# Who issues the stores of new v into the ring: SyncE or ScalarE

## The chip, the cores and the metric

The kernel runs on one core of a Trainium2 chip. Its engines are TensorE (PE, with its weight loads PEld), VectorE (DVE), ScalarE (ACT), GpSimd (POOL) and SyncE (SP, which computes nothing and issues DMAs). Each engine takes its own instructions in order; between engines a semaphore is incremented by one instruction and waited for by another. The metric is the device time of one execution in microseconds.

## The reference, cut to what matters

Four layers run one after the other on 16 sequences of 256 tokens and 128 channels: a gated recurrence, a mixture of experts, a linear attention, and a six-layer local attention transformer. The last one is the part that the change touches and nearly all of the time. Each of its six layers does this:

```
def attn_layer(x, Wqkv, qs, ksc, Wo):
    q, k, v = jnp.split(x @ Wqkv, 3, -1)            # 16 heads of 64
    q, k = l2norm(q) * qs, l2norm(k) * ksc          # then both are rotated
    ...
    out = local_attention(q, k, v)                  # window of 32, and the window before
    return out @ Wo

def local_attention(q, k, v):
    bk2, bv2 = look(bk), look(bv)                   # this window's keys and values, and the last one's
    sim = jnp.einsum('bhwie,bhwje->bhwij', bq, bk2) * QK_SCALE
    attn = jax.nn.softmax(jnp.where(mask, -big, sim), -1)
    return jnp.einsum('bhwij,bhwje->bhwie', attn, bv2)
```

A feed-forward layer with a GELU gate follows each attention layer.

## The kernel before

The tokens are cut into 8 windows of 32. A unit u is one window of one layer (48 units), a group n is one unit's share of four sequences, 128 rows (192 groups). One loop over groups, written once per engine, is a software pipeline: in round n the engines project q, k and v of group n (`proj`, six matmul groups into PSUM banks), score group n-2 (`sim`), take exponents of n-3 (`exps`), turn probabilities and multiply by values of n-4 (`probs`, `values`), and project the output of n-5 (`out_proj`). The feed-forward work of an earlier unit is spread over the four rounds of a unit; q4 = n % 4 says which pieces stand in a round. The order on each engine is written out by hand; nothing is reordered by a scheduler.

The keys and values of the current and the previous window lie in a ring. The ring of v is `V2` in `big1`: the rows of one window lie at partitions 64*par + 32*(c % 2), where par is the parity of the head and c the window. The projection of v gives 128 rows in which the four sequences lie below one another, so v has to move across partitions. ACT copies each half of it from PSUM into the staging tile `vst` (`v_out(n, par)`, L1255), which increments the semaphore a_vst, and four DMAs of 32 partitions by 2 KB each (L340) carry it from `vst` into `V2`. They increment d_v of the group's place in the unit. `values` waits for these DMAs four rounds later, and the next group's first `v_out` waits for them before it overwrites `vst`.

On ACT the part of a round around it is: `v_out(n, 0)`, `square(n, 2)`, `turned_k(n - 2, 0)`, `square(n, 3)`, `turned_k(n - 2, 1)`, `out_turned(n - 4, 0)`, `v_out(n, 1)`, and at the start of the next round `out_turned(n - 4, 1)`, in one round of four a GELU, the two `turned_q(n, h)` (L1262), and then squares and `probs` copies in turn. PE's order in a round is: `turn_q` of the round before, `proj(n, 0)`, `probs(n - 4, 0)` (L592), `proj(n, 1)`, `probs(n - 4, 1)`, `out_proj`, feed-forward pieces, `values` (L608), `proj(n, 4)` (the first half of v), `proj(n, 2)`, `turn_k`, `proj(n, 3)`, `turn_k`, `mask`, `proj(n, 5)`, `sim` (L581), `turn_q(n, h)` (L546). Banks 2 and 3 are shared by v, the turned q and k and the probabilities, so each user waits until ACT has emptied the bank for the one before: `probs(n - 4, 0)` takes bank 3 after `turned_q(n - 1, 0)` has read it.

SP issues all other loads of this stage too: rotation tables once per unit (L323), and new weights once per layer into `stage` (L336, L343), which ACT and DVE split into a high and a low part (`weights`, L1240).

Of the kernel before, what the change touches and what calls it, by code (L numbers as in the profile page):

```python
# [16 lines left out]
NC, W = 8, 32  # L17
N = NB * W
DEPTH, HEADS, DH = 6, 16, 64
# [7 lines left out]
TURN = (0, 1, 4, 2, 3, 5)  # L27
# [124 lines left out]
def program(nc, x_d, kc_d, wa_d, wb_d, ba_d, tab_d, qs_d, wqkv_d, wo_d, w1_d, w2_d, vec_d, we_d, out_d, keep_d, xsort_d, ysort_d):  # L152
    with ExitStack() as ctx:
# [11 lines left out]
        stage = sb("stage", [P, 2, 512])  # L165
# [21 lines left out]
        vst = sb("vst", [P, 2, 512])  # L187
# [28 lines left out]
        s = sems  # L216
# [33 lines left out]
        V2 = big1[:, :].rearrange("p (b n) -> p b n", b=NB)  # L250
# [17 lines left out]
        def _(eng):  # L268
            q = Lane(eng, sems)
# [14 lines left out]
            for what, c, j in chunk_order("SP"):  # L284
# [14 lines left out]
                elif what == "wt" and j < 4:  # L299
                    q.wait_ge("v_w", j + 1)  # L300
                    m = TURN[j + 2]
# [8 lines left out]
            for n in range(NG + 32):  # L310
                u, i = n // 4, n % 4
                l, c = unit(u)
                if n < NG:
                    if n % 32 == 5 and n > 32:
                        q.wait_ge("p_wo", n - 5)
                        eng.dma_start(wo[:, :, :], wo_d[l]).then_inc(s["d_wo"], 16)
                    if i == 0 and u + 1 < NU:
                        if c == NC - 1:
                            q.wait_ge("g_tab", u - NC + 1)
                            eng.dma_start(qsb[:, (l + 1) % 2, :, :], qs_d[l + 1]).then_inc(s["d_qs"], 16)  # L320
                        q.wait_ge("v_k", 16 * u)
                        q.wait_ge("g_tab", u)
                        eng.dma_start(tab[:, (u + 1) % 2, :, :], tab_d[(u + 1) % NC]).then_inc(s[f"d_tab{(u + 1) % 2}"], 16)  # L323
                    if n % 32 == 8 and l + 1 < DEPTH:
                        q.wait_ge("v_w", 6 * (l + 1))
                        for j in range(2):
                            m = TURN[j]
                            eng.dma_start(stage[:, j, :], wqkv_d[l + 1, :, 512 * m:512 * m + 512]).then_inc(s[f"d_st{j}"], 16)
                    q.wait_ge("p_av", n - 3)
                    q.wait_ge("g_zero", 2)  # L330
                    for par in range(2):
                        if n % 32 == 31 and l + 1 < DEPTH:
                            for j in (0, 1) if par == 0 else (2,):
                                m = TURN[j + 2]
                                q.wait_ge("v_w", 6 * (l + 1) + j + 1)
                                eng.dma_start(stage[:, j % 2, :], wqkv_d[l + 1, :, 512 * m:512 * m + 512]).then_inc(s[f"d_st{j % 2}"], 16)  # L336
                        q.wait_ge("a_vst", 2 * n + par + 1)
                        rows = 64 * par + 32 * (c % 2)
                        for b in range(4):
                            eng.dma_start(V2[rows:rows + 32, 4 * i + b, :], vst[32 * b:32 * b + 32, par, :]).then_inc(s[f"d_v{i}"], 16)  # L340
                    if n % 32 == 31 and l + 1 < DEPTH:
                        q.wait_ge("v_w", 6 * (l + 1) + 4)
                        eng.dma_start(stage[:, 1, :], wqkv_d[l + 1, :, 512 * TURN[5]:512 * TURN[5] + 512]).then_inc(s["d_st1"], 16)  # L343
                if n % 32 == 24 and l + 1 < DEPTH:
                    q.wait_ge("v_w1", l + 1)
                    eng.dma_start(w1, w1_d[l + 1]).then_inc(s["d_ffn"], 16)
                if n % 32 == 16 and 32 < n < NG:
                    q.wait_ge("p_fw", 8 * l)
                    eng.dma_start(w2, w2_d[l]).then_inc(s["d_down"], 16)
                v = u - 3  # L350
                if i == 0 and NU - NC <= v < NU:
                    q.wait_ge("v_w", 6 * DEPTH)
                    q.wait_ge("v_back", v - (NU - NC) - 1)
                    q.wait_ge("d_keep", 16 * NC)
                    eng.dma_start(stage[:, v % 2, :], keep_d[:, v % NC, :]).then_inc(s[f"d_back{v % 2}"], 16)
                v = u - 7
                if i == 0 and NU - NC <= v < NU:
                    q.wait_ge("v_out", v - (NU - NC) + 1)
                    eng.dma_start(out_d[:, v % NC, :], Xr[:, v % NC, :]).then_inc(s["d_out"], 16)
# [769 lines left out]
        def _(eng):  # L1129
            ac = Lane(eng, sems)  # L1130
# [26 lines left out]
            for n in range(2):  # L1157
                rows = slice(W * n, W * n + W)
                eng.activation(idb[rows, :].rearrange("p (b t) -> p b t", b=4), kc[rows, rows].unsqueeze(1).to_broadcast([W, 4, W]), ACT.Copy,
                               scale=1.0, bias=0.0).then_inc(s["a_mb"], 1)  # L1160
            for what, c, j in chunk_order("ACT"):
# [30 lines left out]
                elif what == "tx":  # L1192
                    n = 4 * c + j
# [4 lines left out]
                elif what == "he":  # L1198
                    k, m = PR * c + j, 256 * min(2, TL - 2 * j)
# [28 lines left out]
                elif what == "wt":  # L1228
                    m = TURN[j]
# [19 lines left out]
            def v_out(g, par):  # L1249
                if not 0 <= g < NG:  # L1250
                    return
                ac.wait_ge("p_proj", 6 * g + TURN.index(4 + par) + 1)
                if g:
                    ac.wait_ge(f"d_v{(g - 1) % 4}", 128 * ((g - 1) // 4 + 1))
                eng.activation(vst[:, par, :], bank[RING["v"][par]][:, :], ACT.Copy, scale=1.0, bias=0.0).then_inc(s["a_vst"], 1)  # L1255

            def turned_q(g, h):
                if not 0 <= g < NG:
# [426 lines left out]
```

## Time and profile before

| | |
|---|---|
| median of 3 runs | 3699.72 us (3698.93 to 3707.35) |
| the profiled execution | 3692.47 us |
| its span, first to last instruction | 3690.6 us |
| around the span | 1.87 us |
| PE busy | 3457.5 us, 94% |
| POOL busy | 2814.9 us, 76% |
| DVE busy | 2807.4 us, 76% |
| ACT busy | 2365.4 us, 64% |
| mean granted TensorE clock | 0.972 |

The profiled execution is 7.3 us (0.2%) below the median of the runs. Busy time counts work on the engine; instructions that wait or issue DMAs are not counted as busy. The attention loop runs from about 590 us to the end of the span; the first of the 384 v copies starts at 589.5 us and the last one, the second of its round and some 3.5 us into it, at 3563.6 us. Between them lie 191 rounds, so a round takes (3563.6 - 3.5 - 589.5) / 191 = 15.55 us.

### The profile page before, as it was taken

What the parts mean: (1) busy time and instruction counts of PE and PEld (TensorE: products, weight loads), DVE (VectorE), ACT (ScalarE), POOL (GpSimd) and SP (SyncE); (2) the same over time, 40 slices, a digit from 0 to 9 for tenths busy, and PEclk for the clock granted to TensorE, in tenths of its full rate; (3) what the DMA queues carried; (4) which work ended last, traced back from release to release, by engine and by line L of the source; (5) the groups of instructions that cost most, each with busy time, mean ns of one, the idle gap of its engine ahead of it and who ended that gap; (6) DMA issues with size and microseconds to landing.
All of it is one profiled execution on the core that took longest, in us unless ns stands there. A gap on an engine that the chain in (4) does not pass through costs nothing.

```text
span 3690.6 us, 148973 instructions
## 1 busy us (share of the span) xinstructions
PE 3457.5 (94%) x64612; PEld 2724.5 (74%) x64612; DVE 2807.4 (76%) x4876; ACT 2365.4 (64%) x4307; POOL 2814.9 (76%) x3470
## 2 busy tenths in 40 slices
PE   4799986999999999999999999999999999999996
PEld 2566644888877888787888778887787877888774
DVE  3487666888887888878888878888788888788762
ACT  3333223677777777777777677777677777777662
POOL 1455547998878888888888788888888888888761
PEclk9799997999999999999999999999999999999998
DMA  3323302211112111111111211111111112111110
GB/s 106 99 89 95 91 24 58 50 40 38 46 49 50 39 42 42 49 42 45 41 40 45 50 50 38 43 42 49 43 46 40 44 40 57 38 43 47 36 37 24
DMA packets 126733, 183.48 MB, mean 50 GB/s; under 512 B 29824, under 2 KB 61440, under 8 KB 126080
## 3 DMA queue, kind: packets, MB, share of 16 engines
q1 hardware_dynamic: 119232, 146.15, 15.8%
q0 software_dynamic: 6848, 27.80, 2.5%
q8 instruction: 511, 8.37, 1.0%
q14 instruction: 142, 1.16, 0.1%
HBM read 59.01 MB, written 14.16 MB: 20 GB/s over the span
## 4 chain that ended last, share of the span: by engine, by line
PE 84%; POOL 5%; DVE 3%; issue 3%; ACT 2%; DMA 1%; SPq 0%; ACTq 0%; POOLq 0%; DVEq 0%
PE bank L536 22%; PE bank L608 10%; PE bank L619 9%; PE bank L581 7%; PE bank L546 5%; PE bank L556 4%; PE bank L592 4%; PE bank L682 3%; PE bank L660 3%; PE bank L671 3%; PE bank L568 2%; PE bank L451 1%; PE bank L511 1%; PE bank L628 1%; PE bank L490 1%
## 5 line engine op out<-in xcount | busy, mean ns | idle before, releaser
L536 PE MATMUL bank<-wqkv,xs 128*128 128x512 f32 x3456 | 1060.9, 422 | 17.2 <-DVE m L957 12.9
L1540 POOL TENSOR_TENSOR m<-m 128x512 f32<-128x512 f32 x576 | 728.7, 1285 | 42.0 <-DVE m L957 39.2
L536 PEld LDWEIGHTS bank<-wqkv,xs 128*128 128x128 f32 x3456 | 582.7, 191 | 146.4 <-issue 57.2
L957 DVE TENSOR_TENSOR m<-bank,tab 128x512 f32<-128x512 f32 x768 | 522.4, 680 | 0.7 <-POOL m L1540 0.3
L1247 ACT ACTIVATE sq<-bank 128x512 f32<-128x512 f32 x768 | 458.5, 597 | 96.9 <-PE bank L536 53.3
L1548 POOL TENSOR_TENSOR S<-S,nw 128x1024 f32<-128x1024 f32 x192 | 383.3, 1996 | 166.0 <-DVE S L988 166.0
L968 DVE TENSOR_REDUCE ss<-sq 128x8 f32<-128x512 f32 x768 | 505.7, 675 | 0.0
L1556 POOL TENSOR_TENSOR S<-S,rs 128x512 f32<-128x512 f32 x384 | 411.0, 1091 | 63.8 <-DVE rs L1002 62.2
L608 PEld LDWEIGHTS bank<-P,big 64*64 64x64 f32 x24576 | 379.3, 135 | 82.0 <-issue 74.6
L955 DVE TENSOR_TENSOR m<-bank,tab 128x512 f32<-128x512 f32 x576 | 392.6, 682 | 56.3 <-ACT sq L1247 41.1
L619 PE MATMUL bank<-OT,wo 128*128 128x128 f32 x3072 | 389.1, 282 | 39.3 <-ACT P L1286 25.9
L608 PE MATMUL bank<-P,big 64*64 64x32 f32 x24576 | 402.1, 220 | 5.0 <-issue 3.8
L1255 ACT ACTIVATE vst<-bank 128x512 f32<-128x512 f32 x384 | 229.6, 598 | 273.2 <-PE bank L536 258.8
L619 PEld LDWEIGHTS bank<-OT,wo 128*128 128x128 f32 x3072 | 370.6, 197 | 43.1 <-issue 42.8
L1262 ACT ACTIVATE qT<-bank 128x512 f32<-128x512 f32 x384 | 209.8, 596 | 246.1 <-PE bank L546 246.1
L1540 POOL TENSOR_TENSOR mk<-mk,m 128x512 f32<-128x512 f32 x192 | 242.4, 1284 | 101.6 <-DVE m L957 101.6
L977 DVE TENSOR_REDUCE mx<-bank 128x8 f32<-128x512 f32 x384 | 247.0, 685 | 89.8 <-PE bank L581 88.5
L581 PEld LDWEIGHTS bank<-big,qT 64*32 64x32 f32 x24576 | 265.8, 105 | 65.2 <-issue 62.9
L581 PE MATMUL bank<-big,qT 64*32 64x64 f32 x24576 | 300.0, 226 | 6.6 <-issue 6.1
L955 DVE TENSOR_TENSOR mk<-bank,tab 128x512 f32<-128x512 f32 x192 | 131.6, 686 | 198.7 <-ACT sq L1247 198.6
L988 DVE TENSOR_TENSOR S<-bank,mx 128x512 f32<-128x512 f32 x384 | 245.4, 680 | 0.0
L995 DVE TENSOR_REDUCE mx<-S 128x16 f32<-128x1024 f32 x192 | 232.4, 1211 | 16.7 <-ACT S L1279 14.0
(232 smaller groups left out, 6463.1 us busy)
## 6 DMA issues: line engine op xcount, KB each, us to landing
big<-vst SPq DMA_DIRECT2D x1536, 64.0 KB, 2.0
stage<-in_wqkv SPq DMA_DIRECT2D x36, 256.0 KB, 3.0
tab<-in_tab SPq DMA_DIRECT2D x48, 128.0 KB, 2.2
xsort<-big SPq DMA_DIRECT2D x4, 960.0 KB, 8.4
big<-xsort SPq DMA_DIRECT2D x12, 256.0 KB, 4.9
ysort<-big SPq DMA_DIRECT2D x12, 256.0 KB, 3.6
wo<-in_wo SPq DMA_DIRECT2D x6, 512.0 KB, 3.8
big<-in_x SPq DMA_DIRECT2D x8, 256.0 KB, 3.4
```

Of the source, the lines that this page charges most:

```text
L536: m = eng.matmul(pb[:, :], xt[a], wqkv[:, z, 512 * part:512 * part + 512], start=(n == 0), stop=(n == 2))
L581: m = eng.matmul(bank[4 + par][32 * b:32 * b + 32, 64 * r:64 * r + 64], qT[rows, g % 2, r, 32 * b:32 * b + 32], kT[rows, r, :, 4 * i + b, ...
L608: m = eng.matmul(bank[6 + par][half:half + 64, 128 * k + 32 * b:128 * k + 32 * b + 32], V2[rows, 4 * i + b, 64 * r:64 * r + 64], P2[rows, ...
L619: m = eng.matmul(pb[:, 0:128], wo[:, r, :], OT[:, g % 2, r, :], start=(r == 0), stop=(r == 7))
L955: eng.tensor_tensor(turned(g, part).rearrange("p (h d) -> p h d", d=DH), pv, ct.unsqueeze(1).to_broadcast([P, 8, DH]), ALU.mult)
L957: eng.tensor_tensor(m2[:, s3, :].rearrange("p (h s d) -> p h s d", s=2, d=DH // 2), pw, sn.rearrange("p (s d) -> p s d", s=2).unsqueeze(1) ...
L968: eng.tensor_reduce(ss[:, g // 2 % 2, a:a + 8], sq[:, part % 2, :].rearrange("p (h d) -> p h d", d=DH), axis=X_AX, op=ALU.add).then_inc(s[ ...
L977: eng.tensor_reduce(mx[:, g % 2, 0, :].rearrange("p (r q) -> p q r", q=2)[:, par], bank[4 + par][:, :].rearrange("p (r k) -> p r k", r=8), ...
L1247: eng.activation(sq[:, part % 2, :], bank[part % 2][:, :], ACT.Square, scale=1.0, bias=0.0).then_inc(s["a_sq"], 1)
L1540: eng.tensor_tensor(turned(g, part), turned(g, part), m2[:, part % 2, :], ALU.add).then_inc(s["g_add"], 1)
L1548: eng.tensor_tensor(S16, S16, nw[:, g // 2 % 2, 1, 32 * (g % 2):32 * (g % 2) + 16].unsqueeze(2).to_broadcast([P, 16, 64]), ALU.mult).then_ ...
L1556: eng.tensor_tensor(S8, S8, rs[:, g % 2, 8 * h:8 * h + 8].unsqueeze(2).to_broadcast([P, 8, 64]), ALU.mult).then_inc(s["g_pn"], 1)
```

## The change

The four DMAs that follow each `v_out` are issued by ACT, in its own program order right behind the copy, instead of by SP. The waits go with them: that `values` of four groups before has finished with the place in the ring (p_av), that the ring has been zeroed (g_zero), and that the copy into `vst` itself has ended (a_vst). The data, the addresses and the semaphores are the same. SP keeps the other loads, and the weight loads of a layer's last round now stand together in its program.

```diff
@@ SP, in the loop over n
-                    q.wait_ge("p_av", n - 3)
-                    q.wait_ge("g_zero", 2)
-                    for par in range(2):
-                        if n % 32 == 31 and l + 1 < DEPTH:
-                            for j in (0, 1) if par == 0 else (2,):
-                                m = TURN[j + 2]
-                                q.wait_ge("v_w", 6 * (l + 1) + j + 1)
-                                eng.dma_start(stage[:, j % 2, :], wqkv_d[l + 1, :, 512 * m:512 * m + 512]).then_inc(s[f"d_st{j % 2}"], 16)
-                        q.wait_ge("a_vst", 2 * n + par + 1)
-                        rows = 64 * par + 32 * (c % 2)
-                        for b in range(4):
-                            eng.dma_start(V2[rows:rows + 32, 4 * i + b, :], vst[32 * b:32 * b + 32, par, :]).then_inc(s[f"d_v{i}"], 16)
+                    if n % 32 == 31 and l + 1 < DEPTH:
+                        for j in range(3):
+                            m = TURN[j + 2]
+                            q.wait_ge("v_w", 6 * (l + 1) + j + 1)
+                            eng.dma_start(stage[:, j % 2, :], wqkv_d[l + 1, :, 512 * m:512 * m + 512]).then_inc(s[f"d_st{j % 2}"], 16)
@@ ACT, v_out(g, par)
                 eng.activation(vst[:, par, :], bank[RING["v"][par]][:, :], ACT.Copy, scale=1.0, bias=0.0).then_inc(s["a_vst"], 1)
+                ac.wait_ge("p_av", g - 3)
+                ac.wait_ge("g_zero", 2)
+                ac.wait_ge("a_vst", 2 * g + par + 1)
+                rows = 64 * par + 32 * (g // 4 % NC % 2)
+                for b in range(4):
+                    eng.dma_start(V2[rows:rows + 32, 4 * (g % 4) + b, :], vst[32 * b:32 * b + 32, par, :]).then_inc(s[f"d_v{g % 4}"], 16)
```

ACT before, in a round with q4 = 1, from the last GELU pieces ahead of the first v copy to the first turned q of the next round (L1255 is the v copy, L1262 the turned q):

```order
L1365 ACTIVATE gg<-bank,vec 128x512 [waits p_fg]
L1255 ACTIVATE vst<-bank 128x512 [waits d_v0,p_proj]
L1247 ACTIVATE sq<-bank 128x512 [waits v_ss,p_proj]
L1273 ACTIVATE big<-bank 128x4x128 [waits p_tk]
L1247 ACTIVATE sq<-bank 128x512 [waits v_ss,p_proj]
L1273 ACTIVATE big<-bank 128x4x128 [waits p_tk]
L1294 ACTIVATE OT<-bank 128x512 [waits p_av,p_wo]
L1255 ACTIVATE vst<-bank 128x512 [waits p_proj]
L1294 ACTIVATE OT<-bank 128x512
L1365 ACTIVATE gg<-bank,vec 85x512 [waits p_fg]
L1262 ACTIVATE qT<-bank 128x512 [waits p_sim,p_tq]
```

The same place on ACT of the changed kernel, from the first v copy on (its lines are numbered 1 or 7 lower; L1254 is the store):

```order
L1248 ACTIVATE vst<-bank 128x512 [waits d_v0,p_proj]
L1254 DMA big<-vst 32x512 [waits a_vst,p_av]
L1254 DMA big<-vst 32x512 x3
L1240 ACTIVATE sq<-bank 128x512 [waits v_ss,p_proj]
L1272 ACTIVATE big<-bank 128x4x128 [waits p_tk]
L1240 ACTIVATE sq<-bank 128x512 [waits v_ss,p_proj]
L1272 ACTIVATE big<-bank 128x4x128 [waits p_tk]
L1293 ACTIVATE OT<-bank 128x512 [waits p_wo]
L1248 ACTIVATE vst<-bank 128x512 [waits p_proj]
L1254 DMA big<-vst 32x512 [waits a_vst]
L1254 DMA big<-vst 32x512 x3
L1293 ACTIVATE OT<-bank 128x512
```

Eight DMA issues and two waits for ACT's own copy now stand between instructions of ACT that stood next to each other; behind the second block the GELU and the turned q follow as before. Over the program ACT has 1536 DMAs more and SP 1536 fewer.

SP before, in the last round of a layer (L336 and L343 are weight loads into `stage`, L340 the stores):

```order
L336 DMA stage<-in_wqkv 128x512 [waits v_w,p_av]
L336 DMA stage<-in_wqkv 128x512 [waits v_w]
L340 DMA big<-vst 32x512 [waits a_vst]
L340 DMA big<-vst 32x512 x3
L336 DMA stage<-in_wqkv 128x512 [waits v_w]
L340 DMA big<-vst 32x512 [waits a_vst]
L340 DMA big<-vst 32x512 x3
L343 DMA stage<-in_wqkv 128x512 [waits v_w]
```

And the same place on SP of the changed kernel, with what stands around it:

```order
L320 DMA qsb<-in_qs 128x256
L323 DMA tab<-in_tab 128x256 [waits g_tab,v_k]
L333 DMA stage<-in_wqkv 128x512 [waits v_w] x3
L336 DMA stage<-in_wqkv 128x512 [waits v_w]
L323 DMA tab<-in_tab 128x256 [waits g_tab,v_k] x2
L316 DMA wo<-in_wo 128x1024 [waits p_wo]
```

The four weight loads no longer stand behind stores and their waits.

## Rows read from the trace of the kernel before

**Rows 1.** Page: busy time, share and count by engine; the last chain by engine

```profile
PE 3457.5 (94%) x64612; PEld 2724.5 (74%) x64612; DVE 2807.4 (76%) x4876; ACT 2365.4 (64%) x4307; POOL 2814.9 (76%) x3470
...
PE 84%; POOL 5%; DVE 3%; issue 3%; ACT 2%; DMA 1%; SPq 0%; ACTq 0%; POOLq 0%; DVEq 0%
```

**Rows 2.** Waits, whole span: waiter and releaser, total us, times, longest

```profile
ACT vst L1255 <- PE bank L536: 258.8, 187, 3.1
ACT qT L1262 <- PE bank L546: 246.1, 199, 4.1
...
ACT wqkv L1240 <- DMA stage<-in_wqkv: 20.5, 10, 3.1
```

**Rows 3.** DMA issues on SP by line, ns min/median/max; last row: us to landing

```profile
L340 SPq DMA_DIRECT2D big<-vst x1536: 507/591/1966, 594.0 to 3566.0; - x192
...
L336 SPq DMA_DIRECT2D stage<-in_wqkv x15: 333/334/1023, 1044.8 to 3052.0; - x15
...
big<-vst SPq DMA_DIRECT2D x1536, 64.0 KB, 2.0
```

**Rows 4.** Timeline of SP: start us, us from first to last end, four stores each

```profile
2012.73 2.41 SPq L340 DMA_DIRECT2D big<-vst  x4
...
2001.88 3.14 SPq L340 DMA_DIRECT2D big<-vst  x4
...
2032.33 3.50 SPq L340 DMA_DIRECT2D big<-vst  x4
```

**Rows 5.** Timeline of ACT in a round with q4 = 1: start us, us, instruction

```profile
2012.06 0.60 ACT L1255 ACTIVATE vst<-bank 128x512 f32<-128x512 f32 x1 [1.00 <-PE bank L536]
2012.77 0.60 ACT L1247 ACTIVATE sq<-bank 128x512 f32<-128x512 f32 x1
...
2015.55 0.60 ACT L1255 ACTIVATE vst<-bank 128x512 f32<-128x512 f32 x1
2016.04 0.59 ACT L1294 ACTIVATE OT<-bank 128x512 f32<-128x512 f32 x1
2016.52 0.68 ACT L1365 ACTIVATE gg<-bank,vec 85x512 f32<-85x512 f32 x1
2018.33 1.09 ACT L1262 ACTIVATE qT<-bank 128x512 f32<-128x512 f32 x2 [1.13 <-PE bank L546]
```

**Rows 6.** Timeline, four rounds: first v copy on ACT, first L592 matmuls on PE

```profile
1997.77 0.60 ACT L1255 ACTIVATE vst<-bank 128x512 f32<-128x512 f32 x1 [0.83 <-PE bank L536]
...
2004.19 0.60 PE L592 MATMUL bank<-kc,S 128*128 128x128 f32 x4
...
2019.27 0.60 PE L592 MATMUL bank<-kc,S 128*128 128x128 f32 x4
...
2027.10 0.60 ACT L1255 ACTIVATE vst<-bank 128x512 f32<-128x512 f32 x1 [1.52 <-PE bank L536]
...
2095.64 0.60 ACT L1255 ACTIVATE vst<-bank 128x512 f32<-128x512 f32 x1 [1.52 <-PE bank L536]
...
2103.19 0.60 PE L592 MATMUL bank<-kc,S 128*128 128x128 f32 x4
...
2113.09 0.60 ACT L1255 ACTIVATE vst<-bank 128x512 f32<-128x512 f32 x1 [1.81 <-PE bank L536]
...
2120.39 0.60 PE L592 MATMUL bank<-kc,S 128*128 128x128 f32 x4
```

**Rows 7.** Timeline of PE behind the second turned k: score matmuls, q transposes

```profile
2016.13 1.57 PE L581 MATMUL bank<-big,qT 64*32 64x64 f32 x128
2017.64 1.09 PE L546 MATMUL bank<-kc,m 128*128 128x128 f32 x8
```

**Rows 8.** Windows: stretch, us, busy PE PEld DVE ACT POOL, PEclk, DMA share, GB/s

```profile
92.00:184.00 92.00, 72.63 (x332) 54.84 (x333) 38.42 (x128) 30.95 (x102) 37.19 (x67) 0.79 0.33 98
...
554.00:600.00 46.00, 24.18 (x57) 11.99 (x58) 21.48 (x29) 10.15 (x21) 29.60 (x36) 0.70 0.23 72
...
1500.00:2000.00 500.00, 489.54 (x10418) 401.30 (x10416) 408.64 (x680) 363.43 (x631) 421.27 (x489) 0.99 0.18 44
```

## The prediction

> **What bounds the kernel now.** I read the page first: PE is busy 94% of the span and makes up 84% of the chain that ended last, ACT is busy 64% [rows 1]. In the attention loop PE is busy 490 of 500 us, ACT 363 [rows 8]. So a round of 15.55 us is PE's work, and ACT has 15.55 - 0.727 x 15.55 = 4.2 us free in it. Then the list of waits, for where ACT's free time lies: two places hold most of it, 258.8 us ahead of the v copies, nearly all ahead of the first of a round (1.35 us in each), and 246.1 us ahead of the turned q (1.28 us) [rows 2]. Both are waits for PE. Between these places ACT runs without a gap: seven instructions from the first v copy at 2012.06 to the second at 2015.55 and the copy behind it [rows 5]. The change puts both its blocks of DMAs into this closed run, and not where ACT waits.
>
> Then the timeline, for what PE waits for at the run's end. The turned q ends the run, and PE's probability transposes (L592) need bank 3, which the first turned q empties. In four rounds, one of each q4, the time from the first v copy to those transposes is 6.42, 7.21, 7.55 and 7.30 us (1997.77 to 2004.19, 2012.06 to 2019.27, 2095.64 to 2103.19, 2113.09 to 2120.39) [rows 5, 6], on average 7.12. The rest of the round, from there to the next v copy, is PE's in-order work: 8.43 us on average, 7.83 from 2019.27 to 2027.10 [rows 6].
>
> **What the change does, part by part.**
>
> The stores leave SP. Nothing waited for them there: what PE reads of the ring is stored four rounds, some 60 us, earlier, and it lands in 2.0 us [rows 3]. That removal is worth nothing to the loop. Only the weight loads of a layer's last round gain, since they no longer queue behind stores. ACT waited 20.5 us for such loads in all five layer changes together [rows 2]; ACT being late now would cover them anyway. I take 15 us off, 20.5 at most, 0 at least.
>
> The waits that move. p_av asks for `values` of four groups before; PE does that right ahead of the projection that the v copy itself waits for, so it is met. g_zero is met after the first round. a_vst is ACT waiting for its own copy: it empties the engine before the first DMA. On SP the first store began 0.07 us after the copy's end (2012.06 + 0.60 = 2012.66, to 2012.73) [rows 4, 5]; I take 0.07 on ACT too. Where ACT had started its next instruction 0.49 us after the copy's start (2015.55 to 2016.04) [rows 5], it now starts 0.60 + 0.07 + the block after it.
>
> The block of four issues. No row shows a DMA issued by ACT. The nearest is the same instruction on SP: 507 / 591 / 1966 ns, and blocks of four of 2.41, 3.14 and 3.50 us [rows 3, 4]; of six blocks that I looked at, four took 2.41. Their mean is (4 x 2.41 + 3.14 + 3.50) / 6 = 2.71 us, 5.43 for the two of a round. I take the mean, because on ACT a long issue is in the path as much as a short one. From below: a weight load's issue, 0.334 us [rows 3], makes 8 x 0.334 + 0.1 of gaps = 2.8 us a round. From above: two blocks of the longest kind, 7.0 us.
>
> Queued behind each block on ACT: behind the first the squares of k (DVE's rotation of k waits for them), the turned k (PE's scores), the output copies (`out_proj`); behind the second the turned q, and through bank 3 everything of PE. The new time from the first v copy to the L592 transposes, with the pieces of rows 5: copy and drain 0.67, block B1, from the square at 2012.77 to the second v copy at 2015.55 unchanged 2.78, copy and drain 0.67, block B2, output copy 0.49, first half of the turned q and its handover 0.55 + 0.07. That is 5.23 + B1 + B2 = 5.23 + 5.43 = 10.66 us, and 11.34 where the 0.68 of a GELU stands in between (q4 = 1). Against before: +4.24, +4.13, +3.11, +3.36, on average +3.71 us a round.
>
> Is PE really ready by then? Its scores need the second turned k, which ends at 0.67 + 2.71 + 2.2 = 5.6 us after the first copy's start; scores and q transposes take 2.2 us (2016.13 to 2018.33) [rows 5, 7], so they are done at 7.9. ACT reaches the turned q at 10.0. PE stands still for about 2 us, ACT no longer waits there. The 1.28 us of rows 2 is thus used up: it is in the sum, since the times before contained it. And the 1.35 us ahead of the first v copy can't be used: it is the time in which ACT waits for `out_proj`, `values` and the v projection, which start only after the L592 transposes that are late. It stays, and so do the 8.43 us. POOL needs 421 / 500 x 15.55 = 13.1 us a round [rows 8], below the new 15.55 + 3.71 = 19.26, so no other engine takes over.
>
> Sum: 191 rounds x 3.71 = +709, less 15, = +694 us. The profiled execution took 3692.47 us (span 3690.6 and 1.87 around it); it is 0.2% below the median of the runs, 3699.72, less than any term here. 3692.5 + 694 = 4386, called 4390 us, 19% slower.
>
> A rule of the Trainium skill speaks against so much. "DMA: Bandwidth & Descriptors", section "Issuing engines are not separate DMA queues", holds that issuing from several engines saves only the sequencer's time for starting the DMA, which is usually small beside the DMA. Rows 3 disagree for this transfer: 0.591 us to issue against 2.0 to land, and four issues take longer than one landing. By that rule the change would be nearly free; by the row it is not.
>
> **The rivals.**
>
> *ACT's gaps take it up.* If the wait for PE shrank as ACT grew, the round would be ACT's own work: 363.43 / 500 x 15.55 = 11.3, plus 5.43, plus four handovers of 0.07 = 17.0 us, +1.46 a round, +279, 3970 us. For it: 36% of ACT is idle [rows 1]. Against it: the idle time lies behind PE work that itself waits for the run.
>
> *Issues on ACT cost less than on SP.* At a weight load's price: 5.23 + 2.8 = 8.03 (8.71 with the GELU) gives +1.61, +1.50, +0.48, +0.73, on average 1.08 a round, +206: 3900 us. For it: the long issues might belong to SP. Against it: same transfer, same queue kind.
>
> *ACT hands the DMA over and goes on: the other side.* If an issue held ACT only for its dispatch, the two blocks would cost 8 issues and the two drains, and the place that pays is the wait ahead of the turned q. It is 1.28 us long; the drains take 2 x 0.18 (0.67 instead of 0.49), so below (1.28 - 0.36) / 8 = 0.115 us an issue nothing reaches PE, and only the gain of the weight loads is left: 3692.5 - 15 = 3678 us, 0.4% faster. Against it: the shortest issue in 1536 is 0.507 us [rows 3]. The skill's "Perfetto Trace Analysis", section "Per-instruction lifecycle: what the profiler-reported window actually captures", lets an engine's sequencer run ahead of it through a queue of instructions, but has a DMA's wait and its issue on the sequencer itself; by that, the drained engine stands idle for the whole block, as I have it.
>
> *The clock falls as well.* With PE idle for a fifth of each round the granted clock may drop: it was 0.99 at 490 of 500 us busy, 0.79 at 73 of 92 and 0.70 at 24 of 46 [rows 8]. New PE busy share: 0.979 x 15.55 / 19.26 = 79%, the share of the stretch with 0.79, though there the idle time came in longer pieces. At 0.90 the 8.43 us grow by a tenth, 0.84 x 191 = +161: 4550 us.
>
> **How the numbers follow.** The forecast, ACT's run in full, 0.72; the clock too, 0.08; gaps take it up, 0.08; cheaper issues, 0.07; handed over and faster, 0.03; no difference (the drains and a small issue cost just cover the gain), 0.02. The unknown cost of an issue sets the range: with both blocks at 2.41 the round grows by 3.10 us, 4270; with both at 3.50 by 5.28, 4690; with a weight load's price 3900. The last is unlikely and left out with the gaps rival; the clock is taken in: 4080 to 4620. Faster by over 0.3% 0.03, within 0.3% (what a measurement of this kernel can't tell from no change) 0.02, slower by over 0.3% 0.95.
>
> **What the profile after would show.** Right: DMA rows on ACT's queue of about 0.59 us, blocks of 2.4 to 3.5 us, each beginning 0.07 us after a v copy's end; 10.7 to 11.3 us from the first v copy to the L592 transposes, and 8.4 from there to the next; PE busy near 80% with its wait on the turned q copies ahead of L592; ACT's wait ahead of the turned q gone and the one ahead of the first v copy still about 1.3 us; SP nearly idle. Wrong: issue rows far from 0.59; a round whose second part shrinks (the gaps rival); a granted clock below 0.97 in the loop; a new wait of DVE or POOL, for instance exponents that come late because the scores do.

## The result, and the profile after

The changed kernel takes 4453.17 us (median of 4 runs, 4445.5 to 4466.38) against 3699.32 us before (3691.2 to 3707.35): a ratio of 1.205, 95% interval 1.203 to 1.207. The forecast was 4390 us in a range of 4080 to 4620, with 0.95 on slower. The profiled execution took 4466.38 us, 774 more than that of before; the sum had +694.

The page of the changed kernel: busy time by engine, then the chain that ended last by engine and by line (L1254 is the store, L1248 the v copy).

```profile
PE 3706.8 (83%) x64612; PEld 2864.2 (64%) x64612; DVE 2815.1 (63%) x4876; ACT 2317.3 (52%) x4307; POOL 2820.9 (63%) x3470
...
PE 52%; ACTq 20%; ACT 14%; issue 7%; POOL 2%; DVE 2%; DMA 1%; POOLq 0%; DVEq 0%
ACTq L1254 20%; PE bank L529 10%; PE bank L601 9%; PE bank L612 8%; PE bank L585 4%; ACT vst L1248 4%; ACT big L1272 4%; PE bank L675 3%; PE bank L539 2%; ACT sq L1240 2%; PE bank L574 2%; PE bank L664 2%; PE bank L653 2%; ACT OT L1293 2%; ACT qT L1261 1%
```

ACT is busy only 52% of the span, less than before [rows 1], and yet a third of the last chain runs through it: 20% through its queue, in the stores alone. Issuing isn't counted as busy, so the busy shares alone show nothing that explains a kernel 20% slower.

The list of waits of the changed kernel (waiter and releaser, total us, times, longest):

```profile
ACT OT L1293 <- issue: 562.4, 188, 4.4
ACT sq L1240 <- issue: 427.8, 149, 4.0
PE bank L529 <- ACT big L1272: 323.8, 185, 3.2
ACT vst L1248 <- PE bank L529: 265.7, 207, 5.6
PE bank L585 <- ACT qT L1261: 174.8, 103, 2.7
PE bank L539 <- ACT gg L1364: 65.2, 42, 3.1
ACT qT L1261 <- PE bank L539: 49.5, 93, 3.0
...
ACT wqkv L1233 <- DMA stage<-in_wqkv: 3.1, 6, 1.3
```

The first two are ACT standing still behind its own issues, 562.4 / 188 = 3.0 us behind the second copy and 2.9 behind the first. ACT's wait ahead of the turned q fell from 246.1 to 49.5 us, that ahead of the v copies stayed (258.8, now 265.7), that for weights fell from 20.5 to 3.1 [rows 2]. PE now waits for ACT in three places, and only the second of them, L585 on the turned q, had been in the forecast. The first and largest is v's second projection waiting for the turned k, the third the q transposes waiting for a GELU.

The issues themselves, by line (ns min/median/max), then us to landing:

```profile
L1254 ACTq DMA_DIRECT2D big<-vst x1536: 513/612/2493, 593.0 to 4336.7; - x192
...
big<-vst ACTq DMA_DIRECT2D x1536, 64.0 KB, 2.0
```

That is SP's 507 / 591 / 1966 and 2.0 us again [rows 3]. One round with q4 = 1 on ACT, to be laid beside [rows 5]:

```profile
2381.16 0.60 ACT L1248 ACTIVATE vst<-bank 128x512 f32<-128x512 f32 x1 [1.00 <-PE bank L529]
2381.84 2.44 ACTq L1254 DMA_DIRECT2D big<-vst  x4
2384.39 0.60 ACT L1240 ACTIVATE sq<-bank 128x512 f32<-128x512 f32 x1 [2.63 <-issue]
...
2386.79 0.64 ACT L1248 ACTIVATE vst<-bank 128x512 f32<-128x512 f32 x1
2387.46 2.44 ACTq L1254 DMA_DIRECT2D big<-vst  x4
2389.95 0.60 ACT L1293 ACTIVATE OT<-bank 128x512 f32<-128x512 f32 x1 [2.52 <-issue]
2390.44 0.67 ACT L1364 ACTIVATE gg<-bank,vec 85x512 f32<-85x512 f32 x1
2391.01 0.59 ACT L1261 ACTIVATE qT<-bank 128x512 f32<-128x512 f32 x1
2391.93 0.60 ACT L1261 ACTIVATE qT<-bank 128x512 f32<-128x512 f32 x1 [0.33 <-PE bank L539]
```

And PE in the same round (L529 is v's second projection and later q's first, L574 the scores, L539 the q transposes, L585 the probability transposes):

```profile
2385.52 0.96 PE L529 MATMUL bank<-wqkv,xs 128*128 128x512 f32 x3 [1.81 <-ACT big L1272]
...
2387.78 2.05 PE L574 MATMUL bank<-big,qT 64*32 64x64 f32 x128
2389.76 0.86 PE L539 MATMUL bank<-kc,m 128*128 128x128 f32 x4
2391.26 0.63 PE L539 MATMUL bank<-kc,m 128*128 128x128 f32 x4 [0.64 <-ACT gg L1364]
2391.65 0.95 PE L529 MATMUL bank<-wqkv,xs 128*128 128x512 f32 x3
2392.43 0.60 PE L585 MATMUL bank<-kc,S 128*128 128x128 f32 x4
```

The turned q goes to ACT at 2391.01, but the probability transposes start 1.42 us later, not 0.62: the second half of the q transposes writes bank 2, which the last GELU (2390.44 + 0.67 = 2391.11) has to empty first, and in PE's order it and a projection stand ahead of them.

The same starts, averaged over 166 ordinary rounds of each trace (the 9th to the 184th without the last two of each layer; each kind of round, q4 = 0 to 3, weighs the same), in us after the round's first v copy. "Rest", the second part of a round, is from the probability transposes (L592, L585 in the changed kernel) to the next first copy. The last three kernels are experiments of the next section:

| kernel | second v copy | scores | q transposes | turned q | prob. transposes (q4 = 0, 1, 2, 3) | rest | round |
|---|---|---|---|---|---|---|---|
| before | 3.75 | 4.02 | 5.55 | 6.25 | 7.21 (6.54, 7.20, 7.73, 7.39) | 8.14 | 15.35 |
| changed | 5.86 | 6.23 | 7.91 | 10.24 | 11.36 (10.95, 12.22, 10.56, 11.72) | 8.23 | 19.59 |
| first block on ACT | 5.85 | 6.22 | 7.89 | 8.76 | 9.92 (9.05, 10.42, 8.49, 11.72) | 8.13 | 18.05 |
| second block on ACT | 3.76 | 4.02 | 5.55 | 8.05 | 9.03 (8.33, 9.96, 9.45, 8.39) | 8.34 | 17.38 |
| first, behind the turned k | 5.82 | 4.02 | 6.57 | 7.27 | 8.40 (8.04, 8.59, 9.07, 7.89) | 8.19 | 16.59 |

### The profile page after: what moved, and what is told of

Its sections match the earlier page's. It is cut to its first block, busy times and chain, and to the rows that moved or that the text cites. A ratio compares the mean times of both kernels' runs of the same rounds, so it can differ in the third digit from the quotient of the medians.

```text
span 4464.6 us, 148786 instructions
## 1 busy us (share of the span) xinstructions
PE 3706.8 (83%) x64612; PEld 2864.2 (64%) x64612; DVE 2815.1 (63%) x4876; ACT 2317.3 (52%) x4307; POOL 2820.9 (63%) x3470
## 4 chain that ended last, share of the span: by engine, by line
PE 52%; ACTq 20%; ACT 14%; issue 7%; POOL 2%; DVE 2%; DMA 1%; POOLq 0%; DVEq 0%
ACTq L1254 20%; PE bank L529 10%; PE bank L601 9%; PE bank L612 8%; PE bank L585 4%; ACT vst L1248 4%; ACT big L1272 4%; PE bank L675 3%; PE bank L539 2%; ACT sq L1240 2%; PE bank L574 2%; PE bank L664 2%; PE bank L653 2%; ACT OT L1293 2%; ACT qT L1261 1%
## 5 line engine op out<-in xcount | busy, mean ns | idle before, releaser
L529 PE MATMUL bank<-wqkv,xs 128*128 128x512 f32 x3456 | 1121.6, 442 | 343.7 <-ACT big L1272 323.8
L529 PEld LDWEIGHTS bank<-wqkv,xs 128*128 128x128 f32 x3456 | 618.5, 202 | 490.6 <-ACT big L1272 367.8
L1293 ACT ACTIVATE OT<-bank 128x512 f32<-128x512 f32 x384 | 235.3, 614 | 564.8 <-issue 562.4
L585 PE MATMUL bank<-kc,S 128*128 128x128 f32 x1536 | 254.6, 293 | 175.2 <-ACT qT L1261 174.8
L1248 ACT ACTIVATE vst<-bank 128x512 f32<-128x512 f32 x384 | 237.3, 618 | 266.5 <-PE bank L529 265.7
L585 PEld LDWEIGHTS bank<-kc,S 128*128 128x128 f32 x1536 | 201.1, 152 | 264.8 <-issue 228.2
L574 PEld LDWEIGHTS bank<-big,qT 64*32 64x32 f32 x24576 | 296.2, 121 | 75.5 <-ACT big L1272 45.4
L574 PE MATMUL bank<-big,qT 64*32 64x64 f32 x24576 | 333.7, 260 | 3.2 <-issue 1.1
L539 PE MATMUL bank<-kc,m 128*128 128x128 f32 x1536 | 277.5, 332 | 69.3 <-ACT gg L1364 65.2
```

What stands on the lines that cost most here:

```text
L529: m = eng.matmul(pb[:, :], xt[a], wqkv[:, z, 512 * part:512 * part + 512], start=(n == 0), stop=(n == 2))
L574: m = eng.matmul(bank[4 + par][32 * b:32 * b + 32, 64 * r:64 * r + 64], qT[rows, g % 2, r, 32 * b:32 * b + 32], kT[rows, r, :, 4 * i + b, ...
L585: m = eng.transpose(pb[:, 128 * j:128 * j + 128], S[:, g % 2, 128 * r:128 * r + 128], ident)
```

## The experiments

All ratios are to runs of the kernel before on the same chip, with 95% intervals.

**The waits alone.** The kernel before with ACT executing the three waits of the change; SP issues.

```diff
                 eng.activation(vst[:, par, :], ...).then_inc(s["a_vst"], 1)
+                ac.wait_ge("p_av", g - 3)
+                ac.wait_ge("g_zero", 2)
+                ac.wait_ge("a_vst", 2 * g + par + 1)
```

> The kernel before, SP issuing all stores, but ACT executes the three waits that the change gave it (its own copy's end above all) behind each v copy; no DMA on ACT. Theory (ACT's closed run from the first v copy to the turned q is in the path, and the issues are what lengthens it): a drain costs at most 0.18 us (0.67 instead of 0.49 us from the copy to what follows), behind the first copy nothing since the square starts 0.71 us after it anyway, behind the second it goes into the 1.28 us wait ahead of the turned q. So 3700 us, within 0.3% of before. Rival (the waits for the copy, not the issues, are what costs: the engine's queue must empty and fill again): two drains of 1 to 2 us each, 3900 to 4450 us.

Measured 3698.05 us, ratio 1.001 (0.999 to 1.002). All of the loss comes with the issues.

**One block each.** ACT issues the four stores behind the first copy (par 0), or those behind the second; SP the others.

```diff
@@ SP
                     for par in range(2):
+                        if par == 0:          # second run: par == 1
+                            continue
@@ ACT, v_out
+                if par == 0:                  # second run: par == 1
+                    ...                       # waits and four issues as in the change
```

> ACT issues the stores of the first v copy of a round only, SP those of the second. Theory: turned k and with it v's second projection, scores and q transposes come 2.7 us later less their slack of about 1.1; the L592 transposes start 8.2 to 9.1 us after the first copy instead of 6.4 to 7.5: +1.25 us a round, 3940 us (3880 to 4010). Rival that each block adds its 2.7 us: half of the change's loss, 4080. Rival that only the sum of ACT's work counts (11.3 + 2.7 is below 15.55 us): 3700.

> ACT issues the stores of the second v copy of a round only, SP those of the first. Theory: ACT's wait ahead of the turned q (1.1 us and more) takes up part of the 2.9 us: L592 starts 8.2, 8.9, 9.2, 8.2 us after the first copy in the four rounds, +1.5 us a round, 3985 us (3920 to 4050). With e2 that makes less than the change's +754: the slack before the turned q is taken twice in the parts and once in the whole. Rival of equal halves: 4080 each. Rival of the sum of ACT's work: 3700.

Measured 4190.36 us, ratio 1.134 (1.131 to 1.138), for the first block, and 4055.4, 1.099 (1.095 to 1.103), for the second. The second is just outside what was expected (at most 4050). The first is far off, 250 us above the expectation and above the rival of halves too. The table says where: the scores come 2.2 us later, not 1.6, and the probability transposes 2.7 us later. Its list of waits has one large entry for PE:

```profile
PE bank L538 <- ACT big L1282: 327.4, 187, 3.1
```

and its timeline of ACT and PE shows the handover:

```profile
2404.26 0.60 ACT L1257 ACTIVATE vst<-bank 128x512 f32<-128x512 f32 x1 [0.99 <-PE bank L538]
2404.94 2.44 ACTq L1264 DMA_DIRECT2D big<-vst  x4
...
2407.97 0.59 ACT L1282 ACTIVATE big<-bank 128x512 f32<-128x512 f32 x1
...
2408.62 0.96 PE L538 MATMUL bank<-wqkv,xs 128*128 128x512 f32 x3 [1.81 <-ACT big L1282]
```

PE needs the first turned k out of bank 3 (done at 2408.56) before it can project the second half of v, and the scores stand behind that in its order. In the trace of before, the same two rows (the first turned k leaving bank 3, then v's second projection into it) read:

```profile
2013.26 0.59 ACT L1273 ACTIVATE big<-bank 128x512 f32<-128x512 f32 x1
...
2014.55 0.96 PE L536 MATMUL bank<-wqkv,xs 128*128 128x512 f32 x3
```

So the slack there is 2014.55 - (2013.26 + 0.59) = 0.70 us, not the 1.1 us between the second turned k and the scores that I had used.

These 0.4 us a round are some 80 us of the 250. Another part stands beside the clock: the mean granted clock of this run was 0.928, of the run with the second block 0.955, and before 0.972. PE's half clock falls in the rounds with q4 = 3 above all. One of them, PE's second projection of v, scores and q transposes, with the turned q on ACT, and a window over it (the third number from the end is PEclk, the granted clock):

```profile
2444.10 0.96 PE L538 MATMUL bank<-wqkv,xs 128*128 128x512 f32 x3 [1.81 <-ACT big L1282]
...
2446.49 2.05 PE L583 MATMUL bank<-big,qT 64*32 64x64 f32 x128
2448.47 1.97 PE L548 MATMUL bank<-kc,m 128*128 128x128 f32 x8
2449.62 0.60 ACT L1271 ACTIVATE qT<-bank 128x512 f32<-128x512 f32 x1 [3.13 <-PE bank L548]
```

```profile
2445.50:2452.00 6.50, 6.50 (x148) 5.93 (x148) 4.33 (x8) 2.43 (x6) 5.50 (x14) 0.50 0.35 81
```

The q transposes take 1.97 us for 1.09 [rows 7], and here ACT waits for them. In the table these rounds come 4.33 us later than before (11.72 for 7.39), the other three kinds 2.16 us on average. If that difference is the clock's, it is 48 x 2.2 = 104 us, an estimate; this run was not repeated with PE kept at work, so the split of the 250 us stays open.

A block delays the turned q in two ways. The first block does it through PE's order (turned q at 8.76 instead of 6.25), the second through ACT's own run (8.05). In the changed kernel PE's delay runs beside ACT's, so both blocks together cost less (+754) than the parts (+497 and +362).

**The first block behind the turned k.** As the run before with the first block alone on ACT, but issued four instructions later, ahead of `out_turned(n - 4, 0)`.

```diff
                 turned_k(n - 2, 1)
+                store(n, 0)                   # waits and four issues of par 0
                 out_turned(n - 4, 0)
```

> The kernel before, with the stores of the first v copy alone issued by ACT, and that behind both turned k. Same four issues a round as in the run that put them right behind the first copy (4190 us). Theory (there the block made PE late: the turned k frees bank 3 for v's second projection, and scores and q transposes follow in order; the slack is 0.65 us): PE is on time now, ACT reaches the turned q 7.2 us after the first copy instead of 6.25, +0.95 us a round, 3875 us (3840 to 3920). Rival (a block costs about the same wherever it stands in the run): 4150 to 4200.

Measured 3909.99 us, 1.057 (1.055 to 1.060). Four instructions further down the same four issues cost +214 instead of +497 us. The granted clock stayed at 0.970 here, so the move takes away both PE's delay and the half clock behind it. In its timeline the scores start at once, and what PE now waits for is the second v copy, which holds bank 3:

```profile
2407.65 0.59 ACT L1285 ACTIVATE big<-bank 128x512 f32<-128x512 f32 x1
2407.65 2.45 ACTq L1267 DMA_DIRECT2D big<-vst  x4
2407.80 0.96 PE L538 MATMUL bank<-wqkv,xs 128*128 128x512 f32 x3
2408.69 1.59 PE L583 MATMUL bank<-big,qT 64*32 64x64 f32 x128
...
2411.37 1.06 PE L548 MATMUL bank<-kc,m 128*128 128x128 f32 x8 [1.09 <-ACT vst L1257]
```

**The changed kernel with the same move,** eight issues on ACT, the first block behind the turned k.

> The changed kernel, with the block of the first v copy moved down ACT's order by four instructions, behind both turned k and ahead of the output copy; eight issues a round in ACT's closed run as before. Theory: ACT's run is as long as in the changed kernel, 10.2 us from the first copy to the turned q, but PE gets the turned k 2.5 us earlier, so scores start 4.0 us after the copy instead of 6.2 and are never late, at whatever clock: L592 at 10.7 us in rounds with q4 = 0, 2 and 3 and about 12 with q4 = 1, where bank 2 still waits for the GELU. Average 11.0 against 11.36, 0.36 x 191 = 70 us less than the change: 4385 us. Rival (PE's path is the one that counts, and with it nearly the whole of the first block): 4160 or less. Rival (the wait before L592 is now one piece of 3 us and the clock falls behind it): 4453 or more.

Measured 4410.37 us, 1.195 (1.191 to 1.199), 43 us less than the changed kernel. It was expected at 4385. Scores at 4.02, turned q at 9.68, L585 at 10.78 after the first copy. As expected in kind: with both blocks in ACT's run, ACT's run is the longer path, and mending PE's gives little. Two things differ from the expectation. The turned q came 0.56 us earlier than in the changed kernel, where no difference was expected, so what was gained isn't all PE's. And the second part of the round took 8.53 us instead of 8.23, with 1.09 us of it at half clock instead of 0.45, so part of the gain was lost again.

**One issue of each block on ACT,** three on SP.

```diff
@@ SP
-                        for b in range(4):
+                        for b in range(1, 4):
@@ ACT, v_out
+                for b in range(1):            # waits as in the change
```

> ACT issues one of the four stores behind each v copy (b = 0), SP the other three. Theory: 0.67 + 0.51 us behind the first copy instead of 0.71, so the turned k is 0.5 us later, about what PE has in hand before v's second projection and the scores (0.7 to 1.1 us); behind the second 0.7 us out of the 1.28 us wait. So 3700 to 3740 us: an issue is free until the slack is gone, then costs its whole 0.6 us. Rival (cost in proportion to the number of issues): a quarter of +754, 3890 us.

Measured 3742.68 us, 1.013 (1.010 to 1.016), 3 us above the expectation and 150 below a share of a quarter. ACT's issue row there, behind the first copy:

```profile
2401.76 0.52 ACTq L1261 DMA_DIRECT2D big<-vst  x1
2402.38 0.60 ACT L1247 ACTIVATE sq<-bank 128x512 f32<-128x512 f32 x1 [0.70 <-PE bank L536]
```

Two issues a round cost 50 us, eight 754: the first issue of each block goes mostly into slack.

**The first block in another place,** the next round's, behind the probability copies, where ACT waits for PE. Eight issues a round as in the change.

```diff
@@ ACT, changed kernel; par 1 is issued behind its copy as before
                 probs(n - 4, 1)
+                store(n - 1, 0)
                 if q4 == 2:
                     shifted(u - 2)
```

> The changed kernel, with the same eight issues on ACT, but those of the first v copy stand in the next round behind the probability copies, ahead of the exponents, where ACT has 1.8, 1.2 or more than 4 us of waits before its next v copy (by q4). Theory (the place decides): the closed run is that of e3, +1.5 us a round, and the next first v copy comes about 1.0 us later on average: +2.5 us a round, 4175 us (4080 to 4280), faster than the change by 6%. Rival (ACT's total decides): no difference, 4453 us. Rival (exponents come late and the probabilities of the next round with them): 4453 or more.

Measured 4173.56 us, 1.130 (1.128 to 1.133). Same engine, same eight issues, 280 us less. L585 starts 9.02 us after the first copy, as with the second block alone (9.03), and the second part takes 9.01 us instead of 8.23. So the place matters as much as the number. The mean granted clock was 0.964 here and 0.921 in the changed kernel; what the clock was worth there (14 to 46 us, below) is much less than 280.

**Sixteen issues instead of eight.**

```diff
                 for b in range(4):
-                    eng.dma_start(V2[rows:rows + 32, ...], vst[32 * b:32 * b + 32, par, :])
+                    for h in (0, 16):
+                        eng.dma_start(V2[rows + h:rows + h + 16, ...], vst[32 * b + h:32 * b + h + 16, par, :])
```

> The changed kernel, with each store of 32 partitions cut in two of 16, so 16 issues a round on ACT for the same bytes. If an issue has a fixed price of about 0.55 us: 8 x 0.55 = +4.4 us a round, +840, 5300 us. If its price follows the bytes or the partitions, issues get as short as half and the time stays at 4453 us.

Measured 5718.44 us, 1.547 (1.545 to 1.550).

```profile
L1255 ACTq DMA_DIRECT2D big<-vst x3072: 514/611/1966, 594.0 to 5598.6; - x192
...
2402.53 5.32 ACTq L1255 DMA_DIRECT2D big<-vst  x8
```

Half the partitions and half the bytes, same price: 611 ns, and a block twice as long. Between these two sizes the price is one of the instruction. That the total came out 420 us above my figure has two parts. An issue costs 0.68 us in the mean of the blocks (5.44 us for eight, averaged), not 0.55: eight more of them a round make 8 x 0.68 = 5.4 us instead of the 4.4 expected, which is some 200 us over the loop. The other 200 are in the second part of the round, which took 9.36 us instead of 8.23, 2.8 us of it at half clock. The mean granted clock of the run was 0.82; that the clock made them was not tried.

**PE kept at work in the wait.** Three runs fill the time ahead of v's second projection with matmuls whose results are overwritten. The first repeats the mask's own bf16 matmuls, six times in place of one, in every round:

```diff
-    eng.matmul(bank[4 + par]..., idb..., mkb..., start=True, stop=...)
+    for again in range(6):
+        eng.matmul(bank[4 + par]..., idb..., mkb..., start=True, stop=...)
```

The other two put eight full 128x128x512 matmuls a round (four for each value of par) ahead of the mask's, the second run in rounds with q4 = 1 and 3, the third with q4 = 3 alone (g is n - 2 here):

```diff
@@ mask(g), ahead of its own matmul into bank[4 + par]
+                    if g % 2 == 1:            # third run: g % 4 == 1
+                        ...
+                        for again in range(4):
+                            eng.matmul(bank[4 + par][:, :], xs[...], wqkv[:, 0, 0:512], start=True, stop=True)
```

> The changed kernel, with PE's mask matmuls (bf16, 0.4 us a pair) issued six times instead of once, 2.0 us of idle repetition of the same writes, ahead of v's second projection, where PE waits about 2 us for ACT. Theory that the loss beyond the forecast (about 0.5 us a round) is the clock that falls to half in this wait in rounds with q4 = 1 and 3, where scores and q transposes then take 4.0 instead of 2.6 us: the granted clock in the loop goes from 0.93 to 0.97 or more and the time to about 4360 us. Rival (the clock doesn't matter, ACT's run is in front): 4453 us or a little more, whatever the clock.

Measured 4529.85 us, 1.225 (1.222 to 1.228): slower by 77 us than the changed kernel, so far above the theory's 4360 and above the rival too, and the mean granted clock in the loop only went from 0.92 to 0.94: rounds with q4 = 3 had 4.1 us at half clock ahead of L585 instead of 5.0. The mean round grew from 19.59 to 19.91 us. Most of all it grew in rounds with q4 = 2, where v's second projection now starts 5.12 us after the first copy instead of 4.41: there the filling outlasts the wait. With so little change in the clock this run decides nothing about what the clock costs.

> The changed kernel, with eight full 128x128x512 matmuls (2.1 us) into the banks of the scores, just ahead of the mask that overwrites them, in rounds with q4 = 1 and 3, where PE waits 1.8 to 2.3 us for ACT and ran at half clock behind it. Theory that the half clock makes PE late in rounds with q4 = 3 (L592 at 11.76 us after the first copy instead of 10.66): the low clock goes away there, 0.25 us a round less on average, 4405 us, mean granted clock of the loop 0.96 or more. Rival (the clock falls for the wait as such or not, but ACT's run is in front anyway): 4453 us, or up to 40 more where the filling runs longer than the wait.

Measured 4468.06 us, 1.208 (1.206 to 1.211). The mean granted clock in the loop rose from 0.92 to 0.96, and the time stayed, as the rival had it: rounds with q4 = 3 fell from 18.31 to 17.50 us, those with q4 = 1 rose from 20.24 to 20.97, with v's second projection 0.35 us later than without the filling. So the last run fills the former alone.

> As the run with eight full matmuls ahead of the mask, but in rounds with q4 = 3 only. There the filling shortened rounds with q4 = 3 from 18.3 to 17.5 us, while rounds with q4 = 1 grew from 20.2 to 21.0. Theory (the half clock costs 0.8 us in each round with q4 = 3, a fifth of a microsecond on average, and the loss in the other rounds came from filling them): 48 x 0.8 = 38 us less than the change, 4415 us (4400 to 4435). Rival (what q4 = 3 gains, the following rounds give back by running at the lower clock instead): 4445 to 4460 us.

Measured 4439.18 us, 1.201 (1.199 to 1.204), beside 1.205 (1.203 to 1.207) of the changed kernel: 14 us less, and the intervals overlap. Windows over the loop, of the changed kernel and of this one (PEclk is the third number from the end):

```profile
590.00:4340.00 3750.00, 3145.93 (x61493) 2509.58 (x61494) 2435.02 (x4030) 2088.01 (x3710) 2516.65 (x2909) 0.92 0.14 35
```

```profile
590.00:4320.00 3730.00, 3182.58 (x62034) 2506.33 (x62034) 2438.67 (x4036) 2083.65 (x3715) 2523.32 (x2919) 0.95 0.14 35
```

The filled rounds, those with q4 = 3, got shorter as expected, on average from 18.31 to 17.36 us, which alone would be 48 x 0.95 = 46 us. The others hardly moved (q4 = 0 unchanged, 1 shorter by 0.1, 2 longer by 0.2 us). So the half clock does make PE late in rounds with q4 = 3. The mean ordinary round went from 19.59 to 19.38 us and the profiled execution from 4466.38 to 4439.92; of the medians 14 us remain: 4439 us is between what was expected (at most 4435) and the rival (at least 4445). What the clock costs the changed kernel in all is not settled: 14 us by the medians, 26 by the profiled executions, up to 46 by the filled rounds.

**The weight loads ahead of the stores,** on SP, in the kernel before.

```diff
@@ SP, n % 32 == 31
+                        for j in range(4):
+                            q.wait_ge("v_w", 6 * (l + 1) + j + 1)
+                            eng.dma_start(stage[:, j % 2, :], ...)
                     for par in range(2):
                         ...                   # the stores of both halves, without loads in between
```

> The kernel before, with SP's four weight loads of a layer's last round ahead of its stores of that round, as they stand after the change. ACT waits for such loads 20.5 us in five places. Theory: 10 to 17 us of it go, 3685 us, 0.3 to 0.5% faster than before. Rival: the stores of that round, now behind waits for weights, or the loads' own landing time keep it: 3700 us.

Measured 3685.45 us, 0.998 (0.997 to 0.999), 8 us less than the kernel before (3693.33 beside it), where 10 to 17 had been expected. The wait fell by half:

```profile
ACT wqkv L1237 <- DMA stage<-in_wqkv: 9.7, 8, 1.5
```

This is the one piece of the change that is worth keeping. By itself it beats the kernel before, by 0.2%.

## Why the prediction was right, and where it was off

**The stores leave SP, worth nothing to the loop; weight loads gain 15 us.** Right in kind. The wait went from 20.5 to 3.1 us. Done alone, the move took 10.8 us off the wait and 8 us off the time, where the sum had 15; what it gave within the change was not measured apart.

**The waits that move.** Right: 0.68 us from the copy's start to the first issue (2381.16 to 2381.84), and nothing where they stand alone (1.001).

**The block.** Right. 612 ns by the median, and 2.77 us a block on average over all 384, against the 2.71 of six blocks on SP (all 384 of SP have 2.75, so the six were a fair sample). Taking SP's row for ACT, and the mean instead of the median for something in the path, were the choices that carried the forecast: with 2.41 it would have been 4270. The rival of cheaper issues and that of a handover fall with this row.

**ACT's run.** Right to 0.2 us. The turned q was forecast at 10.0 us after the first copy (10.7 with the GELU) and came at 10.12 without and 10.60 with it, 10.24 over all four kinds. That this run is the path that counts is shown by the changed kernel with its first block moved behind the turned k: the scores were on time there (4.02), and 43 us were gained of 754. The rival that ACT's gaps take it up falls: ACT's wait ahead of the first v copy is what it was, and moving a block into that gap is what gained 280 us.

**"Is PE really ready by then?"** This step failed. It put the scores at 5.7 us and the q transposes' end at 7.9 us. The scores came at 6.23; the q transposes began at 7.91 only and ended a microsecond or more later. The step overlooked that v's second projection stands ahead of the scores and waits for bank 3; that bank 2 holds the GELU's input in rounds with q4 = 1; and that PE could be at half clock. It cost little because ACT's run was longer still, by the forecast's own figures 2.1 us longer (10.0 against 7.9). That the margin sufficed is partly luck: with the first block alone, where PE's path is in front, the same kind of step came out 250 us low. In rounds with q4 = 0 and 2 the sum of 10.66 us was met (10.95, 10.56). With q4 = 1 it was 12.22 for 11.34: the bank 2 handover above, 1.42 for 0.62 us in that round, is nearly all of that. The run with the second block alone has it too (9.96 where 8.9 was expected), at a mean granted clock of 0.955. With q4 = 3 it was 11.72 for 10.66; PE was at half clock there, and with PE kept at work in these rounds it came at 10.83. Windows over one such round of the changed kernel:

```profile
2426.50:2431.00 4.50, 4.48 (x140) 3.82 (x140) 4.43 (x9) 2.90 (x6) 2.51 (x2) 0.64 0.06 15
2431.00:2435.00 4.00, 4.00 (x21) 3.56 (x18) 2.98 (x5) 1.80 (x4) 2.62 (x9) 0.55 0.74 214
```

and PE's timeline there, scores, q transposes and q's first projection:

```profile
2426.47 0.96 PE L529 MATMUL bank<-wqkv,xs 128*128 128x512 f32 x3 [2.27 <-ACT big L1272]
...
2429.00 2.05 PE L574 MATMUL bank<-big,qT 64*32 64x64 f32 x128
2430.99 1.97 PE L539 MATMUL bank<-kc,m 128*128 128x128 f32 x8
2432.61 1.63 PE L529 MATMUL bank<-wqkv,xs 128*128 128x512 f32 x3
```

PE stood still for 2.27 us ahead of its projection at 2426.47, the granted clock fell behind that, and the transposes that took 1.09 us [rows 7] take 1.97. On average over the four kinds the excess is (0.29 + 0.88 - 0.10 + 1.06) / 4 = 0.53 us, and an ordinary round grew by 19.59 - 15.35 = 4.24 instead of 3.71. (Two small differences cancel here: the four rounds that were measured before the change were 0.09 us shorter in their first part than the average, 7.12 for 7.21, and the second part grew by 0.09.) Over all 191 rounds the growth is less: the stores began between 594.0 and 3566.0 us before and between 593.0 and 4336.7 after, (3743.7 - 2972.0) / 191 = 4.04 us, since the last two rounds of each layer, 11 in all, grew by only 1.5 us each (19.6 to 21.1), and the first eight by 2.5. Part of what the 11 had was waiting for weights. 191 x 4.04 = 772 us is the 774 measured; the sum had 709 less 15.

**The clock.** In the forecast it was a rival, at 0.90 with +161 us. The clock did fall, to 0.92 in the loop from 0.99 at the busy stretch [rows 8], which the prediction itself had named as a sign of being wrong (below 0.97). An ordinary round of the changed kernel has on average 2.4 us at half clock ahead of the probability transposes, where PE waits for ACT anyway except in rounds with q4 = 3, and 0.45 us behind them. The second part, where it would have cost most, stayed at 8.23 us against 8.14, and with the clock at 0.95 the time moved by 14 us. So the rival had the event right and its place wrong. The clock is not where most of the time went, but what it did cost was missing from the sum.

**The range.** Its ends, 4080 and 4620, follow from no term: the prediction's own bounds for an issue and a block gave 3900 and 4690, its rival of the clock 4550.

## What to carry to other kernels

An instruction that issues a DMA costs its engine's queue its full time, here 0.6 us for 64 KB or 32 KB alike, and no busy share shows it. Put it on an engine whose lateness nobody sees, and count the issues, not the bytes. Take the price from a row of the same kind of transfer: the weight loads, 256 KB each, took 0.33 us to issue [rows 3]. Where it must stand on a busy engine, look for the place where that engine waits anyway: the same eight issues cost 754 or 480 us by place, and two of them, one behind each copy, 50. To price an insertion, follow not only the engine's own next consumer but each PSUM bank that it frees late, since the other engine's order carries the delay on. And ask what the new wait does to TensorE's clock: where its work behind the wait is in the path, as with the first block alone, half clock makes it longer.

## What the runs showed of the hardware

A block that had no need to wait for the copy began while the preceding activation was still running: both start at 2407.65 in the run with the first block behind the turned k, and the next activation starts 2.49 us later. So here an issue ran beside work already handed to the engine, and kept only new work out. A store issued by ACT has the price that it has on SP (612 and 591 ns, both 2.0 us to landing). About one issue in ten takes over 0.9 us on either engine, 160 of 1536 on SP and 156 on ACT; what makes them long was not looked into.
